# A 16-batch linear-attention and mixture-of-experts kernel: the router's product in four groups of columns, transposes by VectorE, new instruction lists

## The reference

```python
q, k, v = elu(ln(x) @ Wq.T) + 1, elu(ln(x) @ Wk.T) + 1, ln(x) @ Wv.T      # 16 heads of 16
out_i = (q_i . sum_{j<=i} k_j v_j) / (q_i . sum_{j<=i} k_j + 1e-8)        # causal linear attention
x = x + out @ Wo.T
h = ln(x)
logits = h @ gate_w.T                                                     # 8 experts
scores = sigmoid(logits); scores_c = scores + bias
# the 2 best of 4 groups of 2 experts, among these the 4 best experts
cw = 2.5 * scores / sum(chosen scores), 0 for the experts not chosen      # [tokens, 8]
y = sum_e cw[:, e] * (silu(h @ Wg[e]) * (h @ Wu[e])) @ Wd[e] + shared expert
x = x + y
```

## Time and profile before

| | |
|---|---|
| median of 3 runs | 1066.31 us (1066.13 to 1067.27) |
| the profiled execution | 1064.54 us, its span 1062.7 us |
| TensorE clock granted | 0.998 of full speed on average |
| busy share of the span | PE 97%, DVE 81%, POOL 49%, ACT 40% |
| DMA engines | 35% busy, 91 GB/s |

### The profile page before, as it was taken

One profiled execution on the slowest core, in us unless ns is written; L12 is line 12 of the kernel. 1 busy time (PEld: TensorE's weight loads), 2 busy tenths in 40 slices (PEclk: granted clock), 3 DMA queues, 4 the chain that ended last, 5 costly groups with the idle time before them and its releaser, 6 DMA issues.

```text
span 1062.7 us, 22269 instructions
## 1 busy us (share of the span) xinstructions
PE 1035.6 (97%) x8481; PEld 878.6 (83%) x8481; DVE 857.4 (81%) x1856; ACT 421.1 (40%) x751; POOL 515.6 (49%) x423
## 2 busy tenths in 40 slices
PE   7899999999999999999999999999999999999998
PEld 6777888888788888878888887888878888888887
DVE  5999978798787979878798897879978798786553
ACT  5544342443435244352443434334342443431222
POOL 4223435535355463544635355463544645353556
PEclk9999999999999999999999999999999999999999
DMA  6001424444252453324434252453425444240512
GB/s 222 2 21 52 99 57 124 81 110 100 56 135 61 110 119 91 100 54 136 82 110 101 56 134 60 110 120 84 106 50 141 81 110 101 56 113 24 135 40 85
DMA packets 234889, 96.46 MB, mean 91 GB/s; under 512 B 161440, under 2 KB 217248, under 8 KB 234784
## 3 DMA queue, kind: packets, MB, share of 16 engines
q1 hardware_dynamic: 234784, 95.04, 35.5%
HBM read 66.57 MB, written 28.44 MB: 89 GB/s over the span
## 4 chain that ended last, share of the span: by engine, by line
PE 48%; DVE 9%; DMA 6%; issue 5%; POOL 4%; ACT 3%; SPq 1%; DVEq 0%; ACTq 0%; POOLq 0%
PE bank L918 30%; PE y_bank L918 11%; PE bank L1025 3%; DMA x_dram<-blocks 2%; PE bank L1039 2%; POOL h_lo L683 2%; DMA expo<-x_dram 2%; POOL et L679 1%; DVE stats L698 1%; ACT h_hi L637 1%; SPq L496 1%; DVE blocks L778 1%; PE bank L1012 1%; DMA cw_all<-cw_dram 1%; DVE et L895 1%
## 5 line engine op out<-in xcount | busy, mean ns | idle before, releaser
L683 POOL TENSOR_TENSOR h_lo<-et,h_hi 128x512 fp32r<-128x512 f32 x144 | 183.2, 1287 | 169.6 <-ACT h_hi L637 169.2
L918 PE MATMUL bank<-xt_hi,wg_hi 128*128 128x512 f32 x576 | 234.6, 407 | 0.5 <-DVE scores L805 0.3
L918 PE MATMUL bank<-xt_hi,wg_lo 128*128 128x512 f32 x576 | 228.9, 397 | 0.0
L918 PE MATMUL bank<-xt_lo,wg_hi 128*128 128x512 f32 x576 | 227.4, 395 | 0.0
L679 POOL TENSOR_TENSOR et<-et,cw_all 128x512 f32<-128x512 f32 x128 | 164.5, 1292 | 99.5 <-DVE et L901 66.1
L805 DVE TENSOR_TENSOR scores<-bank,cst 128x512 f32<-128x512 f32 x256 | 163.9, 679 | 25.4 <-PE bank L1025 20.5
L637 ACT ACTIVATE h_hi<-et 128x512 fp32r<-128x512 f32 x144 | 88.6, 627 | 212.7 <-POOL et L679 184.8
L918 PE MATMUL y_bank<-wd_hi,h_hi 128*128 128x256 f32 x576 | 164.8, 286 | 0.1
L895 DVE SCALAR_TENSOR_TENSOR et<-et,bank 128x512 f32<-128x512 f32 x144 | 97.0, 682 | 81.1 <-ACT et L628 79.7
L918 PE MATMUL y_bank<-wd_lo,h_hi 128*128 128x256 f32 x576 | 161.1, 280 | 0.0
L918 PE MATMUL y_bank<-wd_hi,h_lo 128*128 128x256 f32 x576 | 161.0, 280 | 0.0
(11 more groups left out here) (130 smaller groups left out, 1918.2 us busy)
## 6 DMA issues: line engine op xcount, KB each, us to landing
cw_all<-cw_dram SPq DMA_DIRECT2D x128, 256.0 KB, 3.7
x_dram<-blocks SPq DMA_DIRECT2D x112, 128.0 KB, 3.3
x_in<-in_x SPq DMA_DIRECT2D x16, 512.0 KB, 5.2
out_y<-x_mid SPq DMA_DIRECT2D x32, 256.0 KB, 3.8
num_t<-x_dram SPq DMA_DIRECT2D x15, 512.0 KB, 4.0
...
k_tok<-k_dram SPq DMA_DIRECT2D x13, 384.0 KB, 3.4
```

The costliest lines, as they stand in the source:

```text
L683: nc.gpsimd.tensor_tensor(h_lo[:, i % HR, :], et[:, i % ET, :], h_hi[:, i % HR, :].bitcast(f32), ALU.subtract).then_inc(h_lo_done, 1)
L918: ins = nc.tensor.matmul(dst, l, r, start=first and n == 0, stop=last and n == 2, skip_group_check=shared)
```

## The change

The router's product is done on unsplit float32 (`num_t` for batches 1 to 15; for batch 0, which is never in `num_t` in transposed form, on `xt_hi` and `xt_lo` as two float32 operands). The weights of the router, padded from 8 to 32 columns, are the stationary operand, the tokens move, and each block of 128 tokens goes to its own 32 partitions of the bank: 8 MATMULs of the code for a batch (16 for batch 0). DVE turns 32 x 32 blocks of that bank into `logit`, and in `rank1` it turns `cw` (now 4 x 32 columns, of which 8 in each 32 are used) into `cw_t`, so that `weights_turn` is gone from PE and ACT. `cw_store` writes 128 rows of 128 instead of 32, and a `cw_load` reads four pieces of 128 elements instead of one of 512. `spread`, which overwrites `num_t`, now waits for the router of the batch before. The split of the router's weights is gone. `beaten` compares in place. All lists and the table of banks are other ones; `FIRST` holds 106 `warm` transposes instead of 79. The steps of a repeated list are the same set except for `weights_turn`.

```diff
@@ STEP, PE (the other lists and BANK change in the same way)
-        inter.1.1 router.0.2 gate.2.2 gate.0.2 up.0.2 down.6.3 gate.1.2 q.0.0 k.0.0 q.1.0 k.1.0 values.2.1
+        scores.3.1 gate.0.2 gate.2.2 router.0.2 values.2.1 values.3.1 up.2.2 down.6.3 q.0.0 up.0.2 q.1.0 k.0.0
...
-        wr_parts = sb("wr_parts", [P, KC, 2, E], f32r)
-        wr_raw = sb("wr_raw", [P, KC, E])
+
+        wr = sb("wr", [P, KC, RG])
...
-        cw = sb("cw", [P, E, SUBS])
-        cw_t = sb("cw_t", [E * SUBS, P])
+        cw = sb("cw", [P, SUBS, RG])
+        cw_t = sb("cw_t", [P, P])
...
-                    sp.wait_ge(drained[BANK["weights_turn", 0]], USES["weights_turn", 0, b])
-                    sp.dma_start(cw_dram[b % 2].rearrange("e (s p) -> (e s) p", p=P), cw_t[:, :])\
-                        .then_inc(cw_stored, 16)
+                    sp.wait_ge(cw_turned, b + 1)
+                    sp.dma_start(cw_dram[b % 2], cw_t[:, :]).then_inc(cw_stored, 16)
...
-                    sp.dma_start(cw_all[:, i % CW, :], cw_dram[b % 2, i].partition_broadcast(P))\
+                    sp.dma_start(cw_all[:, i % CW, :].rearrange("p (g t) -> p g t", t=P),
+                                 cw_dram[b % 2].rearrange("(g e) t -> e g t", e=RG)[i].partition_broadcast(P))\
...
-                elif name == "weights_turn":
-                    act.wait_ge(filled, FILLED["weights_turn", 0, b])
-                    if b > 0:
-                        act.wait_ge(cw_stored, 16 * b)
-                    nc.scalar.activation(cw_t[:, :], bank[BANK["weights_turn", 0]][0:E * SUBS, 0:P], ACT.Copy)\
-                        .then_inc(drained[BANK["weights_turn", 0]], 1)
...
-                link(nc.vector.tensor_tensor(eq[:, :, :, :], other, own_v, ALU.is_equal))
-                link(nc.vector.tensor_tensor(cmp[:, :, :, 1, :], eq[:, :, :, :],
+                link(nc.vector.tensor_tensor(cmp[:, :, :, 1, :], other, own_v, ALU.is_equal))
+                link(nc.vector.tensor_tensor(cmp[:, :, :, 1, :], cmp[:, :, :, 1, :],
...
-                    if b > 0:
+                    if b - 1 in TURNED[1]:
+                        wait_filled(dve, "turn", 2, b - 1)
+                        wait_filled(dve, "turn", 3, b - 1)
+                    elif b > 0:
                         wait_normal(dve, 1, b - 1)
+                        wait_filled(dve, "router", 0, b - 1)
...
-                    nc.vector.tensor_reduce(
-                        logit[:, :, :].rearrange("p s e -> p (s e)"),
-                        bank[BANK["router", 0]][:, 0:SUBS * 2 * E].rearrange("p (s t e) -> p s e t", s=SUBS, t=2),
-                        AX.X, ALU.add).then_inc(drained[BANK["router", 0]], 1)
+                    nc.vector.transpose(logit[:, :, :].rearrange("p s e -> p (s e)"), bank[BANK["router", 0]][:, 0:P])\
+                        .then_inc(drained[BANK["router", 0]], 1)
...
+                    dve.wait_ge(cw_ready, CW_READY["rank1", 0, b])
+                    if b > 0:
+                        dve.wait_ge(cw_stored, 16 * b)
+                    nc.vector.transpose(cw_t[:, :], cw[:, :, :].rearrange("p s e -> p (s e)")).then_inc(cw_turned, 1)
...
-                    for s in range(SUBS):
-                        ss = slice(s * P, (s + 1) * P)
-                        dst = bk[:, s * 2 * E:(s + 1) * 2 * E]
+
+                    whole = [t.bitcast(f32) for t in (XT[0][:, :, :], XT[1][:, :, :])] if b in TURNED[1] else [None]
+                    for n, src in enumerate(whole):
                         for kc in range(KC):
-                            nc.tensor.matmul(dst, XT[0][:, kc, ss],
-                                             wr_parts[:, kc, :, :].rearrange("p t e -> p (t e)"),
-                                             start=(s == 0 and kc == 0), stop=False, skip_group_check=True)
-                            last = nc.tensor.matmul(dst[:, 0:E], XT[1][:, kc, ss], wr_parts[:, kc, 0, :],
-                                                    start=False, stop=(kc == KC - 1), skip_group_check=True)
+                            for s in range(SUBS):
+                                rhs = landed[1][:, s, kc, :] if src is None else src[:, kc, s * P:(s + 1) * P]
+                                last = nc.tensor.matmul(bk[RG * s:RG * s + RG, 0:P], wr[:, kc, :], rhs,
+                                                        start=(n == 0 and kc == 0),
+                                                        stop=(n == len(whole) - 1 and kc == KC - 1),
+                                                        skip_group_check=True)
                     last.then_inc(filled, 1)
-                elif name == "weights_turn":
-                    pe.wait_ge(cw_ready, CW_READY["rank1", 0, b])
-                    nc.tensor.transpose(bk[0:E * SUBS, 0:P], cw[:, :, :].rearrange("p e s -> p (e s)"), ident)\
-                        .then_inc(filled, 1)
```

More of the change, by code:

```diff
@@ L33 @@
     "PE": """
[L34 to L38 removed]
+        down.0.3 up.5.3 wo.0.2 state.1.1 wo.1.2 gate.8.3 down.1.3 scores.1.1 down.2.3 up.8.3 gate.7.3 up.7.3
@@ L50 @@
+        weigh.2.2 weigh.1.2 split.1.2 qk.1.0
         """,
     "DVE": """
-        wo.0.2 wo.1.2 ln2_stats.0.2 mask.6.1 mask.5.1 ln2_apply.0.2 blocks.1.2 mask.7.1 gate.7.3 mask.4.1
-        ln1_stats.0.0 gate.6.3 up.7.3 up.6.3 gate.8.3 state.1.1 blocks.0.0 up.8.3 mask.10.1 mask.11.1 mask.9.1
-        mask.8.1 mask.15.1 mask.14.1 mask.13.1 router.0.2 gate.0.2 spread.0.1 up.0.2 mult.0.1 gate.2.2
-        route.0.2 rank0.0.2 mask.12.1 q.0.0 k.0.0 rank1.0.2 gate.1.2 spread.1.1 q.1.0 mult.1.1 up.1.2 k.1.0
@@ L71 @@
[L71 to L73 removed]
+        turn.0.0 turn.1.0 warm.17.0 q.0.0 v.0.0 k.0.0 k.1.0 q.1.0 k_turn.0.0 v.1.0 warm.12.0 scores.0.0
+        warm.14.0 scores.1.0 state.0.0 values.0.0 k_turn.1.0 turn.1.1 inter.0.0 turn.0.1 warm.10.0 scores.2.0
```

239 lines of the change are left out of this document (113 added, 126 removed).

## The result

The changed kernel takes 1268.07 us (median of 4 executions, 1255.87 to 1272.77), the kernel before in the same comparison 1066.22 (1064.5 to 1067.27). The ratio is 1.188, 95% interval 1.178 to 1.197: 19% slower, where 2% faster was forecast. The profiled execution has a span of 1262.1 us.

The account below looks back on a forecast made before the run. PE, busy 97%, was taken to bound the repeated lists. Router 21.0 plus `weights_turn` 1.9, minus mode changes 1.3 and `warm` 1.5, saves 20.1 us: 1066.3 to 1046.2, stated as 1045; range 1034 to 1056.

Parts of the forecast that it names:

- The DMA paragraph: Loads of `cw_all` in 512 B pieces: no longer than today's 3.7 us, or at most one more us.
- So I leave the stalls as they are: PE's stalls, 1 to 2 us of a repeated list, were taken as unchanged by the new lists.
- Rival 1: New lists stall more: a list 0.5 to 1.3 us worse costs 7 to 17 us, giving 1050 to 1062; 13%.
- The stretch that I followed: PE and DVE from `gate.2` to `v.1`: the wait at `spread` costs DVE 0.8 us, PE nothing, with 1.9 us to spare.
- the sum itself: Gains and costs added on PE's time: 21.0 + 1.9 - 1.3 - 1.5 = 20.1 us saved.
- The router on PE: Router product at 0.45 us a batch instead of 1.79, 0.9 for batch 0: gain 21.0 us, range -0.5 to 21.
- rival 3: Router's four column groups not side by side: not at all, 1066 to 1067, 2%; half way, 1056, 3%.
- `weights_turn` and changes of mode: On PE: dropping `weights_turn` gains 1.9 us; 15 more passages between split and unsplit float32 cost 1.3 us.
- `FIRST`: 27 more `warm` transposes there: half of 3.0 us, so -1.5 us; the router's 0.9 us saving there may vanish in waits.
- DVE none: New transposes on DVE, about 0.25 us each, +0.3 us per batch, 5 us over the run: no cost to the time.
- the first term: The router's gain on PE, 21.0 us; by the skill's 81 ns an instruction it would be some 8 us.
- Rival 4: PE's router waits up to 2.7 us per list for late DVE masks: 35 us lost against 20, so 1081; 4%.

Follow-up runs that it names:

- e1: Changed kernel with each expert's weights stored as one 2 KB row in DRAM, so a load reads 2 KB pieces instead of 512 B; 1073.58 us, ratio 1.0085.
- e5: e1 with the lists and banks of the kernel before, minus the `weights_turn` steps; new router, transposes and in-place comparisons stay; 1057.95 us, ratio 0.9937.
- e16: e13 without its added wait for batch 0; 1056.81 us, ratio 0.9913.
- e13: e1 with one added wait, by which POOL starts no split before `ln2_apply` has ended; 1059.03 us, ratio 0.9946.
- e11: e5 with three more passes of the router's product ahead of it in each of the 16 batches; 1065.50 us, ratio 1.0019.
- e9: e5 with DVE emptying `gate.2` before `spread` and ACT taking both halves of the next rows together; 1059.88 us, ratio 0.9962.

## Why the prediction was wrong

The forecast of 1045 was missed by 223 us: 194 by the loads (after against e1), 16 by an overlap that the new lists brought (e1 against e5), and the last 13 because less of PE's saved work came out as time (e5 against 1045).

- **The DMA paragraph failed, with 194 of the 202 us** (after against e1). I priced a load in pieces by the nearest row of equal piece size, `k_tok` with 512 B, and put "no longer, or at most one more us". `k_tok` still lands in 3.4 us. The rows share the size of a piece but not the distance between pieces or the broadcast, and I had not asked at which addresses the new loads read. By the medians it was 6.4 us more for each of 128 loads, and for every transfer near them. The cover that I named, POOL at 49%, was not the point: the queue's other work was late, `k_dram`, `x_in`, `out_y`, and those PE and DVE wait for. By the two windows, of the 165 us between e1 and after in the repeated lists 111 are idle time of PE and 54 its longer busy time at the lower clock.
- **"So I leave the stalls as they are" failed, with 15.6 us** (e1 against e5). Rival 1 had its size (7 to 17 us, 13%), not its cause. The stretch that I followed held for PE, which the router doesn't stall. On DVE `spread` waits longer than forecast, 1.3 us each time, and in e1 20.3 us in 13 with 2.6 as the longest; e16 still has 20.1 of it and the shortest lists, so it isn't the cause. What failed is the premise that an instruction lasts as long in the new order as in the old. `ln2_apply` lasted 0.65 us instead of 0.41, since POOL's splits had come to stand beside it, and made the mask for `gate.6` late. One added wait took 14.5 of the 15.6 us back (e13).
- **A third error lay in the sum itself**: PE's saved time was counted in full because PE was 97% busy. With no slow loads and no overlap, 6 of 23 us came out with the old lists (e5) and 8.5 of 20 with the new ones (e16). Stalls of 1 us a list hid that a chain through SP, ACT and DVE to `q.0` ran nearly level with PE, and 1.2 us less on PE put it in front. e11 shows that there was such a second chain: 21 us of work put back cost 7.5. Which one it is, is read from one place of the trace, and e9 shows that behind it stand the masks of `values`.
- **The router on PE was right**: 0.46 us, by 0.45; the four groups run side by side, so rival 3 falls. In the 13 lists it was worth 15.7 us up to the next step, 17.4 forecast; the change of mode now stands behind it.
- **`weights_turn` and changes of mode** were near nothing together (0.3 us in the lists of e5), **`FIRST`** came out 1.5 us longer, where the terms of the sum that fall into it come to about nothing.
- **DVE none** was right for the new operations, 283 and 312 ns where 250 was estimated, not for the old ones.
- **Three small workings don't come out, and decide nothing.** The 0.09 us for a change of mode is read behind a router whose factors are split like those of the gate after it, so that row shows no such change; no run shows the term of 1.3 us by itself. With 1.8 us for a router and twice that for batch 0 the low end of the first term is -2, not -0.5. The "some 8 us" for the first term counts batch 0 once; counted twice, as in the sum, it is 6.5.
- **Rival 4** did not occur: no mask was a whole `scores` late at the router. The slower side came from a rival that I had not written down.
